# A state-space block with a routed feed-forward part: routing moved beside the scans, results scattered to the place that each row carries, and combined without gathers

## The reference

```python
h = layernorm(x) * (1 + ca) + sa                       # modulation by sequence
gate = sigmoid(h @ W2 + b2)
u = sigmoid(causal_conv4(h @ W1 + b1) + conv_b)        # 256 channels
# selective scan, 16 states for each channel:  h = exp(delta*A)*h + delta*B*u;  y = sum(h*C)
x = x + ga * ((selective_scan(u) + u*D) * gate @ Wo + bo)
h = layernorm(x) * (1 + cb) + sb
probs = softmax(h @ router.T)                          # 8 experts, the best 2 of a token are kept
y = sum over the token's 2 experts e of  p_e * ((silu(h @ G_e.T) * (h @ U_e.T)) @ D_e.T)     # inner width 352
out = x + gb * y
```

## Time and profile before

| | us |
|---|---|
| median of 3 runs | 880.84 |
| the profiled execution | 880.26 |
| its span (first to last instruction) | 878.5 |
| scans, first to last start (L1233) | 74.7 to 603.9 |
| last scan's end to tile 0's L1323 | 32.4 |
| tiles 0 to 78, from L1323 to L1323 | 207.5 |
| tile 78's L1323 to the end of the span | 33.4 |

### The profile page before, as it was taken

How to read it: one execution, slowest core, us unless ns; L and a number is a source line. 1 busy time by engine, 2 the same in 40 slices (tenths; PEclk the granted TensorE clock), 3 DMA queues, 4 the chain that set the end, 5 groups by cost and what they waited for, 6 DMA issues and landing times. The chain is left out here.

```text
span 878.5 us, 14696 instructions
## 1 busy us (share of the span) xinstructions
PE 701.2 (80%) x4707; PEld 576.9 (66%) x4707; DVE 565.4 (64%) x992; ACT 579.6 (66%) x1056; POOL 533.1 (61%) x465
## 2 busy tenths in 40 slices
PE   3757979979969969879987897886288999987750
PEld 2334757766857766657766676675278999987740
DVE  2045687689688779579769769898336445534562
ACT  2257888788788798798788879992256465643310
POOL 1005889669779679869778987699400240035665
PEclk9968989989989979989988997997599999998985
DMA  5090211211211112112211121222111232222332
GB/s 164 0 289 33 98 48 49 98 48 48 98 49 48 57 60 102 62 55 97 62 54 61 56 109 55 96 71 87 42 43 45 63 95 67 62 73 77 108 103 75
DMA packets 45034, 66.10 MB, mean 75 GB/s; under 512 B 7136, under 2 KB 36768, under 8 KB 40864
## 3 DMA queue, kind: packets, MB, share of 16 engines
q1 hardware_dynamic: 39456, 54.15, 18.3%
q0 software_dynamic: 4352, 8.92, 3.4%
q10 hardware_dynamic: 1152, 2.10, 0.7%
HBM read 50.86 MB, written 14.29 MB: 74 GB/s over the span
## 5 line engine op out<-in xcount | busy, mean ns | idle before, releaser
L472 POOL TENSOR_TENSOR ring<-ring,Cb 128x1024 f32<-128x1024 f32 x128 | 302.7, 2367 | 54.4 <-DVE ring L1233 49.1
L514 PE MATMUL psum<-ident,S 128*128 128x128 f32 x1024 | 171.0, 293 | 66.1 <-DVE ring L1233 35.9
L514 PEld LDWEIGHTS psum<-ident,S 128*128 128x128 f32 x1024 | 129.1, 152 | 141.4 <-issue 63.7
L514 PE MATMUL psum<-ident,ring 128*128 128x128 f32 x1056 | 168.6, 292 | 31.5 <-DVE ring L1335 14.7
L915 ACT ACTIVATE dA<-delta,A 128x512 f32<-128x512 f32 x256 | 176.1, 712 | 1.3 <-DVE ring L1233 1.2
L907 ACT ACTIVATE S<-duT,BT 128x256 f32<-128x256 f32 x376 | 162.9, 498 | 10.9 <-issue 10.9
L1233 DVE TENSOR_TENSOR_SCAN ring<-dA,psum 128x512 f32<-128x512 f32 x128 | 150.7, 1207 | 19.2 <-PE psum L514 13.8
L1233 DVE TENSOR_TENSOR_SCAN ring<-dA,state,psum 128x512 f32<-128x512 f32 x128 | 158.2, 1267 | 6.5 <-PE psum L514 5.3
L514 PEld LDWEIGHTS psum<-ident,ring 128*128 128x128 f32 x1056 | 135.6, 152 | 34.3 <-issue 24.9
L511 PE MATMUL psum<-dA,Cb 128*128 128x128 f32 x948 | 123.9, 282 | 0.8 <-issue 0.8
L418 POOL DMA_INDIRECT token_table<-h2r,pos x64 | 63.6, 994 | 90.4 <-PE psum L511 76.9
(11 more groups left out here) (180 smaller groups left out, 839.2 us busy)
## 6 DMA issues: line engine op xcount, KB each, us to landing
Cb<-c_rows SPq DMA_DIRECT2D x32, 1024.0 KB, 4.7
dA<-token_table SPq DMA_DIRECT2D x79, 64.0 KB
result_table<-dA SPq DMA_DIRECT2D x79, 64.0 KB
xT<-in_xT SPq DMA_DIRECT2D x4, 512.0 KB, 5.4
out_T<-xT ACTq DMA_DIRECT2D x8, 256.0 KB
token_table<-zeros SPq DMA_DIRECT2D x1, 1472.0 KB, 12.8
gateup_w<-in_gate SPq DMA_DIRECT2D x1, 1408.0 KB, 9.2
gateup_w<-in_up SPq DMA_DIRECT2D x1, 1408.0 KB, 10.1
```

Of the source, the lines that this page charges most:

```text
L472: nc.gpsimd.tensor_tensor(ring[:, k % RING], ring[:, k % RING], Cb[:, group_ % 2, own, :].unsqueeze(1).to_broadcast([P, HALVES, BANK]), AL ...
L514: return nc.tensor.matmul(out, block_in, ident[0:block_in.shape[0], 0:block_in.shape[0]], is_transpose=True, start=start, stop=True, skip_ ...
```

## The change

- `positions` and `prefix` run for each segment of the first three sequences, in gap 7 of windows 2 to 7, on 4 chunks in place of 8; the last sequence keeps one call. Eight scatters go into each of windows 2 to 7 (gaps 9, 14, 20, 26).
- `shared_table` is cut into eleven pieces in gaps 9 to 19 of window 7 (13 instructions; scratch in PSUM). The computation of the results' places is gone.
- A row of the token tables is 136 floats in place of 128; float 128 holds the number of the row's result (choice x 4096 + token). `h2r` has a copy for each choice, so ScalarE copies 1024 elements a partition in place of 512, and GpSimd adds the number (`add_places`).
- The whole shared table is cleared first, with a large number in float 128, by 26 DMAs of 8 tiles (544 B a row): 2 ahead of the loop of windows and 3 behind each of the eight `load_rows` of the first two; 3 more clear the last table in window 3. The eight indirect writes of zeros are gone. The gate and up weights are loaded in window 2, the down weights at the start of window 7 (into the softplus buffers).
- The tiles' buffers are moved to `uT`, `xc`, `S` and to other PSUM banks; most waits for the end of the scans are gone, and TensorE waits for the last y only at tile 1's up product.
- For each tile GpSimd reads the places (`read_places`, 128x1) and scatters the tile's results by an indirect DMA (79 in place of SyncE's 79 stores) to a results table in the order of tokens. Rows that only fill a tile go aside. The last sequence's rows are scattered by tiles 18, 21, ... 39, in the same program order.
- SyncE loads the results of 512 tokens by two plain DMAs of 256 KB: the first four segments behind load 64, two more behind loads 72 and 76, the last two when all 79 scatters have landed. The 64 gathers are gone.
- `pool_chunks`: GpSimd takes 8 chunks less in window 2 and 8 more in window 7; ScalarE the other way.

```diff
@@ -54,7 +55,7 @@
 def pool_chunks(k):
 
     s = k // NSTATE
-    return 1 + k % 2 if s < 3 else int(s < SEGS - 1)
+    return 1 + k % 2 if s < 2 else k % 2 if s == SEGS - 1 else 1
...
-        down_w = S[:, :, :, :].rearrange("p r c m -> p (r c m)").rearrange("p (c m) -> p c m", c=NIN)
+        down_w = soft[:, :, :, :].rearrange("p k a t -> p (k a t)").rearrange("p (c m) -> p c m", c=NIN)
...
-        odd = dA[:, :, :].rearrange("p r t -> p (r t)")
-        xs, xsT, ob = tiles_of(odd, 0, XS_SLOTS), tiles_of(odd, 4 * P, 2), tiles_of(odd, 6 * P, XS_SLOTS)
-        cb_all = Cb[:, :, :, :].rearrange("p r n t -> p (r n t)")
-        silu, innerT = (tiles_of(cb_all, 2 * k * NIN * P, 2, NIN * P) for k in range(2))
-        both_w = tiles_of(cb_all, 4 * NIN * P, 2, INTER + NIN * P)
+        front_all = uT[:, :, :].rearrange("p c m -> p (c m)")
+        xs, xsT = tiles_of(front_all, 0, XS_SLOTS, ROW), tiles_of(front_all, (XS_SLOTS + 1) * P, 2)
+        ob = tiles_of(xc[0], 0, XS_SLOTS)
+        s_all = S[:, :, :, :].rearrange("p r c m -> p (r c m)")
+        silu, innerT = (tiles_of(s_all, 2 * k * NIN * P, 2, NIN * P) for k in range(2))
+        both_w = tiles_of(s_all, 4 * NIN * P, 2, INTER + NIN * P)
...
-        PX, PM = bank(0)[:, 0:P], bank(7)
+        PX, PM = bank(6)[:, 0:P], bank(7)
 
         def PG(k):
-            return bank(1 + k % 2)
+            return bank(2 + k % 2)
 
         def PU(k):
-            return bank(3 + k % 2)
+            return bank((4, 1)[k % 2])
 
         def PO(k):
-            return bank(5 + k % 2)[:, 0:P]
+            return bank((5, 0)[k % 2])[:, 0:P]
...
+            f = window - 2
+            return f if 0 <= f < SHARED_SEGS else SHARED_SEGS if f == SEGS - 1 else None
...
+            def clear(i):
+
+
+                table_, piece, tiles = (token_rows[0], i, EXPERTS * REGION // P + SPARE_TILES) if i < SHARED_CLEARS else (
+                    token_rows[1], i - SHARED_CLEARS, LAST_TILES)
+                first = piece * CLEAR_TILES
+                n = min(CLEAR_TILES, tiles - first)
+                sp.dma_start(table_[first * P:(first + n) * P, :].rearrange("(k p) h -> p k h", p=P),
+                             zeros[:, :].unsqueeze(1).to_broadcast([P, n, ROW])).then_inc(table_cleared, 16)
+
+            sp.wait_ge(zeroed, 2)
             per_seg = NSTATE // C_GROUP
+            early = SHARED_CLEARS - 2 * per_seg * 3
+            for i in range(early):
...
+                if s == 2:
+                    for k, weights in enumerate((gate_d, up_d)):
+                        sp.dma_start(experts_w[:, :, k, :], weights.rearrange("h (e i) -> h e i", e=EXPERTS)
+                                     ).then_inc(loaded["gateup"], 16)
+                if s == 3:
+                    for i in range(SHARED_CLEARS, CLEARS):
+                        clear(i)
+                if s == SEGS - 1:
+                    sp.wait_ge(delta_ready, SEGS * HALVES)
+                    for c, (i0, k) in enumerate(INNER):
+                        sp.dma_start(down_w[0:k, c, :].rearrange("i (e h) -> i e h", e=EXPERTS),
+                                     down_d.rearrange("(e i) h -> i e h", e=EXPERTS)[i0:i0 + k, :, :]
+                                     ).then_inc(loaded["down"], 16)
                 for group_ in range(s * per_seg + 2, (s + 1) * per_seg + 2):
                     if group_ < SEGS * per_seg:
                         load_rows(group_)
-
-            sp.wait_ge(turned_in, STEPS * HALVES)
-            for c, (i0, k) in enumerate(INNER):
-                sp.dma_start(down_w[0:k, c, :].rearrange("i (e h) -> i e h", e=EXPERTS),
-                             down_d.rearrange("(e i) h -> i e h", e=EXPERTS)[i0:i0 + k, :, :]).then_inc(loaded["down"], 16)
-            sp.wait_ge(scanned, STEPS * HALVES)
-
+                    if s < 2:
+                        for i in range(3):
+                            clear(early + (group_ - 2) * 3 + i)
...
+            def load_results(h):
+
+                at = h % (GATH_SLOTS // CS)
+                wait(sp, mixed, TOPK * CS * (h - GATH_SLOTS // CS + 1))
+                for j in range(TOPK):
+                    first = j * NTOK + h * BANK
+                    sp.dma_start(gath[:, at * CS:(at + 1) * CS, j, :],
+                                 results[first:first + BANK, :].rearrange("(c p) h -> p c h", p=P)).then_inc(results_loaded[at], 16)
+
+            def results_given(tiles):
+                for k in range(XS_SLOTS):
+                    sp.wait_ge(given[k], 16 * len(range(k, tiles, XS_SLOTS)))
...
+                if t == SHARED_TILES + 8:
+                    results_given(SHARED_TILES)
+                    sp.wait_ge(summed, STEPS * HALVES)
+                    for h in range(GATH_SLOTS // CS):
+                        load_results(h)
+                if t in (SHARED_TILES + 16, SHARED_TILES + 20):
+                    load_results((t - SHARED_TILES) // CS)
+            results_given(TILES)
+            for h in range(SHARED_SEGS, SEGS):
+                load_results(h)
...
+            def add_places(call, f):
+
+                b, g = divmod(f, SEG)
+                cut_ = slice(0, CH) if call == SHARED_SEGS else slice(g * CS, (g + 1) * CS)
+                for half_ in range(SEG) if call == SHARED_SEGS else (g,):
+                    wait(pool, written[half_], writes(b))
+                nc.gpsimd.tensor_scalar(h2r[:, :, cut_, HID], place_f[:, :, cut_], float(b * SEQ), None, ALU.add
+                                        ).then_inc(places_ready, 1)
...
-            for g in range(SEG):
-                pool.wait_ge(written[g], writes(SHARED))
-            pool.wait_ge(group, PAD_STEP)
-            for e in range(EXPERTS):
-                nc.gpsimd.indirect_dma_start(xs_d[0], bass.IndirectOffsetOnAxis(ap=pad[:, e:e + 1], axis=0),
-                                             zeros[:, :], None).then_inc(padded, 16)
...
-                    for j in range(TOPK):
-                        i = (b * TOPK + j) * CH + c
-                        nc.gpsimd.indirect_dma_start(gath[:, (b * CH + c) % GATH_SLOTS, j, :], None, ys_d[1 - shared],
-                                                     bass.IndirectOffsetOnAxis(ap=pos_g[:, i:i + 1], axis=0)
-                                                     ).then_inc(gathered[(b * CH + c) % GATH_SLOTS], 16)
+            def read_places(t):
+
+                slot, rnd = t % XS_SLOTS, t // XS_SLOTS
+                pool.wait_ge(xs_loaded[slot], 16 * (rnd + 1))
+                wait(pool, given[slot], 16 * (rnd - 1))
+                nc.gpsimd.tensor_scalar(result_at[:, t % (2 * XS_SLOTS):t % (2 * XS_SLOTS) + 1], xs[:, slot, HID:HID + 1],
+                                        aside[:, t:t + 1], None, ALU.min).then_inc(places_read, 1)
+
+            add_places(SHARED_SEGS, SEGS - 1)
+            for t in range(2):
+                read_places(t)
+            for t in range(TILES):
+                if t + 2 < TILES:
+                    read_places(t + 2)
+                c, rest = divmod(t - TAIL_TILES - 1, 3)
+                if rest == 0 and 0 <= c < CH:
+                    if c == 0:
+                        scatter_ready(SHARED_SEGS, SEGS - 1)
+                    scatter(BATCH - 1, c)
+                pool.wait_ge(places_read, t + 1)
+                pool.wait_ge(o_read, t + 1)
+                nc.gpsimd.indirect_dma_start(results,
+                                             bass.IndirectOffsetOnAxis(ap=result_at[:, t % (2 * XS_SLOTS):t % (2 * XS_SLOTS) + 1],
+                                                                       axis=0),
+                                             ob[:, t % XS_SLOTS, :], None).then_inc(given[t % XS_SLOTS], 16)
...
+                if k == 1:
+                    pe.wait_ge(y_out, SEGS)
...
-                    nc.scalar.copy(h2r[:, g * CS:(g + 1) * CS, :].rearrange("p c h -> p (c h)"), FT).then_inc(read["rows"], 1)
+                    nc.scalar.copy(h2r[:, :, g * CS:(g + 1) * CS, 0:HID],
+                                   FT.rearrange("p (c h) -> p c h", c=CS).unsqueeze(1).to_broadcast([P, TOPK, CS, HID])
+                                   ).then_inc(read["rows"], 1)
...
+            def shared_table(gap):
+
+                s = [{9: 0, 10: 1, 11: 3, 12: 5, 13: 6, 14: 7, 15: 8, 16: 9, 17: 10, 18: 11, 19: 12}[gap]]
+                if s[0]:
+                    dve.wait_ge(group, s[0])
...
+                if gap == 9:
+                    dve.wait_ge(read["prefix"], SHARED_SEGS)
+                    then(V.tensor_tensor(count, starts[:, :], region_f[:, :], ALU.subtract))
...
+                if gap == 14:
+                    shape = [P, SHARED_TILES, EXPERTS]
+                    then(V.tensor_tensor(pt, tile_f[:, :].unsqueeze(2).to_broadcast(shape),
+                                         ends[:, :].unsqueeze(1).to_broadcast(shape), ALU.is_ge))
...
-                    wait(dve, ys_stored[slot], 16 * (rnd + (-1 if par < 2 else 0)))
```

(7 more changed lines are left out.)

349 lines of the change are left out of this document (161 added, 188 removed).

## The result

The changed kernel takes 852.88 us (median of 4 runs, 850.9 to 858.19), the kernel before 880.42 beside it (4 runs, 879.98 to 881.38): a ratio of 0.9695, 95% interval 0.965 to 0.9741, so 27.5 us are gained where 42 were forecast. 852.88 lies in the range of 818 to 872. The profiled execution has a span of 850.2 us against 878.5.

The account below looks back on a forecast made before the run. Scan windows were balanced with no engine full; afterwards TensorE idled at the boundary, and gathers on GpSimd paced the last tiles and end. Terms +4 - 20 + 2 + 9 + 0 - 22 - 15 = -42 gave 838 us, range 818 to 872.

Parts of the forecast that it names:

- Scans: Up to the last scan's end: added scatters, moved chunks, prefix chains and table pieces cost +4 us, bounds -4 and +12.
- Boundary: Last scan's end to tile 0's product: 12.4 us against 32.4, -20; if GpSimd's last product stays late, 8 us go.
- Tiles 0 to 17: Tiles beside the last segment's tail: a result scatter each, some late signals; +2 us, bounds 0 and +8.
- Tiles 18 to 41: Tiles with result scatters and the last sequence's scatters: GpSimd full; +9 us, between +1 and +19.
- Tiles 42 to 59: Tiles with one GpSimd issue in 2.14 us: 0 us, upper bound +4.
- Tiles 59 to 78: Tiles formerly beside gathers: steps fall from 3.42 to 2.27 us, -22; 0 if the lateness has another cause.
- End: Tile 78's product to the end, without gathers: 18.5 us against 33.4, -15, bounds -18 and -8.
- A: Tiles 59 to 78: gathers did not make the stalls, so no gain there; 860 us, chance 0.12.
- B: Steps 17 to 78: GpSimd's issues hold back TensorE's signals at every tile, +19 us there; 870 us, chance 0.12.
- C: All 78 tile steps: result scatters close a ring, pace 3.42 us; slower from mean 3.06; 908 us, chance 0.08.
- D: Windows 0 and 1: clears delay eight loads of C by 5 us each, +40; 878 us, chance 0.03.
- E: Boundary: tile 0 starts no earlier, ScalarE reaching it only behind a late y copy, +20; 858 us, chance 0.03.

Follow-up runs that it names:

- computation in place: Changed kernel with each of the last sequence's 16 scatters replaced by a GpSimd multiplication, its results not computed; 842.45 us beside the changed kernel's 853.25.
- prompt condition: Batches whose traces have VectorE's copy at most 0.37 us behind its transposition's start in tiles 20 to 41; kernel before 869.07 and 869.13 us, changed kernel 845.19.
- late condition: Runs where that copy starts up to 1.26 us late in the kernel before, up to 5.49 in the changed one; 880.42 and 881.16 us against 852.88 and 853.25.
- second batch: Follow-up runs in the late condition, both kernels rerun unchanged among them: kernel before 881.16 us, changed kernel 853.25.
- the remedy for GpSimd's load: Changed kernel with each tile's places read on VectorE instead of GpSimd: 836.12 us, prompt condition; with single scatters and spread loads added, 855.71 us, late condition.
- third batch: Follow-up runs in the prompt condition, both kernels rerun unchanged among them: kernel before 869.13 us, changed kernel 845.19.

## Why the prediction was right, and where it was off

The measured time lies inside the range, and also inside its narrower part (818 to 860) that does without the rivals. The stages and the direction of every large term came out as forecast; five of the seven terms cost more or gave less than they promised, two gave a little more: 14 us less gain in all.

1. *Scans, +4; measured +5.0.* Inside its bounds, the parts only partly right, and the closeness is in part luck: in the changed kernel's other two traces the last scan ended at 612.8 and 614.4, 8 to 11 us later than in the three traces of the kernel before (603.4 to 605.2). Window 2 took +3.9 where +2 was taken, and not by the chunks; window 7 took +2.4 by the chunks that GpSimd gained there, forecast as -1 from them and +2 from the table. Of the two operations of the table with two SBUF inputs one, the comparison, fell beside a product:

```profile
579.54 2.52 DVE L1247 TENSOR_TENSOR psum<-tile_f,ends 128x448 f32<-128x448 f32 x1
```

GpSimd's pair of products ran from 576.89 to 581.55 and the comparison, begun 0.3 us behind the start of the second, ended 0.5 us behind it, as L1169 did; operations of the same table with an operand in PSUM took 0.14 to 0.61 us. The other, the count (L1231, 0.15 us at 570.22), ended as the next product began. By the rule of the Trainium skill's page "SBUF — State Buffer", section "SBUF: two separate sides", whichever of the two starts first gets the shared ports for the whole instruction; the trace agrees for this comparison. For L1169 the order does not fit so well: the profile has its start at 609.16, 0.66 us ahead of the products that it ended behind the earlier trace rows.
2. *Boundary, -20; -18.3.* The path is the one foretold. The last product, 5.2 us behind the scan and not 2.4, is the term's own "if" and more than covers the 1.7 us. The prediction had that product "no longer" behind scatters, and overlooked segment 5's scatters in gap 26.
3. *Tiles 0 to 17, +2; -1,* 1 us under its bounds of 0 and +8: the tail's chain shows no loss to GpSimd's issues.
4. *Tiles 18 to 41, +9; +17.3, inside its bounds. This is the step that was mis-sized most.* It took the middle between GpSimd merely full and the full lateness of the signals, "since a result's wait on VectorE breaks the row of issues every few tiles". The runs put 4 to 5 us on GpSimd's time (57.7 with computation in place; 58.4 in the prompt condition) and 10 to 13 on the signals. The reason for the middle did not hold: GpSimd did wait for VectorE's copy of a result (4 times, 10.6 us in the changed kernel's first trace), but in the timelines results wait for the late copy and then come in one row, so that a stall seems to make itself worse; this is a reading, not tested by itself. The small read, taken as 0.2 us, is 0.29 with 0.17 ahead of the issue behind it. With its own upper bound, +19, the sum would have been -32.
5. *Tiles 42 to 59, 0; -0.5.* One issue a tile, with a read in between, costs 0.9 us at most even in the late condition (36.9 against 36.0 in the second batch).
6. *Tiles 59 to 78, -22; -18.1.* Behind the loads the steps are 2.21 us on average, where 2.27 was forecast: most take 2.12, some 2.2 to 2.6. The term had "VectorE may wait 3 us once"; one step took 6.92, 4.8 over the others, because four segments were loaded in one go. Spreading the loads gave 3.7 to 5.6 us back.
7. *End, -15; -12.6.* The order of events is right: last scatter at 832.90, loads issued at 835.28, then sums. The last scatter comes 3.5 us behind tile 78's product instead of 2.8; the rest, 1.6 us, lies behind it.

Of the rivals, A (gathers did not make the stalls) fell in the late condition, where their removal gave 18 us. In the prompt condition it describes those tiles, which run at 43.4 us beside the gathers, and there the gain came at the end instead. Terms 6 and 7 have -37 together and measured -31 in the late condition, -17.5 in the prompt one; that the prompt 845.2 lies in the range as well, though it stands for a smaller gain, is luck: the kernel before was 12 us faster there. B was right about the cause and wrong about its reach: not at every tile, only in rows. C did not come about: the mean pace of the 78 steps is 2.63 us, where it needed 3.06. D and E did not occur: windows 0 and 1 take 61.6 and 66.7 us, as in one of three traces of the kernel before (61.6 and 66.8), and tile 0 came 13.4 us earlier.

## What to carry to other kernels

An engine that only issues DMAs can slow others that wait for nothing from it; look for it where readers wait although the writer has ended, and look at the issues that stand in an unbroken row, not only at their sum. Loads for a later stage that share a queue with a per-tile load go in one at a time. An edit made for one condition should be tried beside the kernel before in each batch: the remedy for GpSimd's load (54.1 us in the prompt condition) was part of a kernel that gained nothing in tiles 17 to 59 where the signals were the trouble.

## What was not expected of the hardware

The same kernel and the same instructions take 869 or 881 us. The granted clock is the same (0.893 to 0.906 in the runs of the kernel before in the second and third batch), each indirect DMA is held 0.94 to 0.95 us in both, and while GpSimd issues a row, a copy behind a transposition starts 0.31 us after it in one, and 4.26 in the other. What sets this condition is open; nothing in the kernels does, since the same kernels were run in both. And the lateness can pass unseen in a total: the changed kernel differs by 8 us between the conditions, the kernel before by 12, in other stretches.
